# Two small writes of the expert choice, made by GpSimd in place of VectorE

## The reference

```python
def _L0_ffn_ref(x, ...):
    h = layernorm(x, ln1_scale, ln1_shift)
    x = x + attention(h, wq, wk, wv, wo, bo)      # causal softmax, 16 heads of 8
    h = layernorm(x, ln2_scale, ln2_shift)
    return x + moe_ff(h, gate_w, w1, w2, w3)

def moe_ff(x, gate_w, w1, w2, w3):
    scores = xf @ gate_w                          # 8 experts
    topk_scores, topk_idx = jax.lax.top_k(scores, 2)
    topk_probs = jax.nn.softmax(topk_scores, axis=-1)
    ...                                           # each token: its two experts, weighted

x = x + 0.5 * _L0_ffn_ref(_layernorm(x), ...)
x = x + _L0_attn_ref(_layernorm(x), ...)          # linear attention
x = x + 0.5 * _L0_ffn_ref(_layernorm(x), ...)
```

## Time and profile before

| | us |
|---|---|
| median of the runs before | 1330.87 |
| the runs | 1331.21, 1330.87, 1326.74 |
| the profiled execution | 1331.67 |
| its span | 1329.9 |

### The profile page before, as it was taken

The page is one execution under the profiler, slowest core; times in us unless marked ns, Lnnn a source line. Parts: engine busy times, 40 slices in busy tenths (PEclk is TensorE's granted clock), DMA queues, the critical chain, the costliest instruction groups (busy, mean ns, idle before and its releaser), DMA issues.

```text
span 1329.9 us, 33572 instructions
## 1 busy us (share of the span) xinstructions
PE 1012.5 (76%) x11497; PEld 753.1 (57%) x11644; DVE 1077.7 (81%) x2383; ACT 771.4 (58%) x1170; POOL 549.9 (41%) x787
## 2 busy tenths in 40 slices
PE   2789888888826998367788858998898888369980
PEld 1567666666624666245455546676676666246660
DVE  5889999999965887687588768899999998458875
ACT  1369787777724555133555534687777787245550
POOL 3402456555663666210033240034465456536660
PEclk9889999999957999566888879999999999579995
DMA  3574233225202332233222206111111010023326
GB/s 101 180 233 126 83 114 112 92 78 159 62 19 73 90 89 65 89 118 116 69 64 65 62 3 202 55 40 36 40 48 44 28 50 18 21 72 88 89 65 197
DMA packets 146339, 111.57 MB, mean 84 GB/s; under 512 B 15664, under 2 KB 140848, under 8 KB 146224
## 3 DMA queue, kind: packets, MB, share of 16 engines
q1 hardware_dynamic: 124080, 78.70, 20.4%
q0 software_dynamic: 9088, 18.76, 4.0%
q10 hardware_dynamic: 13056, 12.59, 2.7%
HBM read 43.49 MB, written 59.82 MB: 78 GB/s over the span
## 4 chain that ended last, share of the span: by engine, by line
DVE 36%; issue 21%; PE 18%; ACT 11%; POOL 8%; DMA 3%; DVEq 1%; ACTq 1%; SPq 1%; POOLq 0%
DVE negm L1031 7%; POOL ys L1434 4%; DVE negm L1035 3%; DVE p_lo L1274 3%; PE banks L422 2%; ACT pf L848 2%; DVE pf L1281 2%; DVE p_lo L1043 2%; DVE x_all L989 2%; ACT p_hi L718 2%; PE banks L457 2%; PE banks L437 1%; ACT yb L741 1%; PE banks L444 1%; DVE p_lo L1047 1%
## 5 line engine op out<-in xcount | busy, mean ns | idle before, releaser
L701 ACT ACTIVATE pf<-banks 128x1536 f32<-128x1536 f32 x128 | 185.8, 1451 | 112.8 <-PE banks L444 110.0
L1043 DVE TENSOR_TENSOR p_lo<-pf,p_hi 128x1536 f16<-128x1536 f32 x128 | 223.9, 1750 | 2.9 <-ACT p_hi L718 1.9
L1434 POOL DMA_INDIRECT ys<-y_out,dest x156 | 151.6, 972 | 115.8 <-ACT y_out L854 90.8
L718 ACT CAST p_hi<-pf 128x1536 f16<-128x1536 f32 x128 | 188.7, 1474 | 2.0
L1385 POOL DMA_INDIRECT xs<-n_all,slot x128 | 166.8, 1303 | 54.9 <-issue 37.6
L1411 POOL TENSOR_SCALAR rs<-mv 128x2 f32<-128x2 f32 x32 | 43.9, 1373 | 334.3 <-DVE mv L1096 278.1
L1031 DVE TENSOR_REDUCE negm<-banks 128x4 f16<-128x1024 f32 x128 | 156.0, 1219 | 18.2 <-PE banks L422 8.9
L444 PEld LDWEIGHTS banks<-ident,negm 128*128 128x128 f16 x1536 | 122.1, 100 | 82.6 <-issue 10.0
L437 PE MATMUL banks<-qst,kst 96*128 96x512 f16 x384 | 151.5, 395 | 2.5 <-ACT pf L701 2.5
L444 PE MATMUL banks<-ident,negm 128*128 128x128 f16 x1536 | 153.1, 223 | 0.3 <-issue 0.2
L422 PE MATMUL banks<-kst,qst 96*128 96x128 f16 x1536 | 129.8, 221 | 30.6 <-DVE negm L1031 20.2
(11 more groups left out here) (197 smaller groups left out, 2471.0 us busy)
## 6 DMA issues: line engine op xcount, KB each, us to landing
xs<-zeros SPq DMA_DIRECT2D x128, 130.0 KB
qk_d<-p_hi ACTq DMA_DIRECT2D x48, 256.0 KB, 2.2
x_nats<-xs SPq DMA_DIRECT2D x78, 130.0 KB
qst<-qk_d SPq DMA_DIRECT2D x192, 48.0 KB
kst<-qk_d SPq DMA_DIRECT2D x48, 192.0 KB
pf<-ys SPq DMA_DIRECT2D x32, 256.0 KB, 3.1
v_hl<-v_all SPq DMA_DIRECT2D x48, 136.0 KB
qk_d<-p_lo SPq DMA_DIRECT2D x96, 64.0 KB, 1.7
```

The lines of the kernel that those rows point to most:

```text
L701: nc.scalar.activation(pf[:, g % 2, :, :, :].rearrange(flat), banks_t[:, :, :].rearrange("p a b -> p (a b)"), ACT.Exp, scale=HD ** -0.5).t ...
L718: nc.scalar.copy(p_hi[:, g % 2, :, :, :].rearrange(flat), pf[:, g % 2, :, :, :].rearrange(flat))\
L1043: nc.vector.tensor_tensor(lo, pf[:, g % 2, :, :, :].rearrange(flat), hi, ALU.subtract)\
L1434: nc.gpsimd.indirect_dma_start(ys, bass.IndirectOffsetOnAxis(ap=dest[:, t % YB, h:h + 1], axis=0), y_out[:, t % YB, h, :], None).then_inc( ...
```

## The change

DVE's `choose` no longer writes `prob` and the column of `n2_all`. A new step on POOL, `keep_route`, does both: the same subtraction, and a copy from `topf` instead of `topi`. It stands directly in front of `slots` of the same batch and raises a new semaphore, `route_kept`, by one per batch over both softmax phases. Since `top` and `topf` have one buffer each, `choose` now waits until `keep_route` of the batch before has read them; the first scatter of a batch waits for its own `keep_route`; and ACT's exponential waits for `route_kept` in place of `top_in`. Where the subtraction stood in `choose`, an `apart` takes over the wait for `max`.

```diff
--- before.py
+++ after.py
@@ -233,7 +233,7 @@
         of_linear = both + "neg_in exp_in full_in k_turn_done k_nat_in state_done state_in carry_done carry_in"
         phases = [dict(shared, n=n, soft=soft, w=0 if soft else 1, back_links=4 if soft else 4,
                        **sems(n, of_soft if soft else of_linear)) for n, soft in enumerate((True, False, True))]
-        e_in = sem("e_in")
+        e_in, route_kept = sem("e_in"), sem("route_kept")
         mixtures = [dict(**sems(f"m{n}", "x_turn x_hi_in h2f_in x_lo_in up_done silu_in hid_in hid_hi_in hid_lo_in down_done "
                                 "y_in dest_in tabled added add_chain chain"), n=n, e_in=e_in,
                          x_loaded=[sem(f"x_loaded_m{n}_{i}") for i in range(XB)],
@@ -263,6 +263,10 @@
         def at_loop(i, n):
 
             return lambda d: ((4 + n + d) % RB, i + (4 + n + d) // RB)
+
+        def kept(ph, n):
+
+            return ph["n"] // 2 * B + n
 
         def fill_no(ph, b, name):
 
@@ -870,7 +874,7 @@
                     hid_high(t)
                 y_read(NTI - 2)
                 y_read(NTI - 1)
-                sc.wait_ge(phases[2 * mixtures.index(m)]["top_in"], B)
+                sc.wait_ge(route_kept, kept(phases[2 * mixtures.index(m)], B))
                 nc.scalar.activation(prob[:, :, 0], prob[:, :, 0], ACT.Exp).then_inc(m["e_in"], 1)
 
             sc.wait_ge(w_in, weights_in)
@@ -1105,17 +1109,17 @@
             def choose(ph, b):
 
                 c = Chain(ve, ph["cv_route"], b * 3)
-                two = bass.ds(2 * b, 2)
                 ve.wait_ge(ph["emptied"], fill_no(ph, b, "b8") + 1)
+                if not (isinstance(b, int) and b == 0):
+                    ve.wait_ge(route_kept, kept(ph, b))
                 apart(ve)
                 for t in range(T):
                     ins = nc.vector.max(top[:, t, :], gates[:, t, :])
                 c.link(ins)
-                nc.vector.tensor_tensor(prob[:, two, 0], top[:, :, 1], top[:, :, 0], ALU.subtract)
+                apart(ve)
                 for t in range(T):
                     ins = nc.vector.max_index(topi[:, t, :], top[:, t, :], gates[:, t, :])
                 c.link(ins)
-                nc.vector.tensor_copy(n2_all[:, two, P + 1], topi[:, :, 0])
                 c.link(nc.vector.tensor_copy(topf[:, :, :], topi[:, :, 0:2]))
                 nc.vector.tensor_tensor(onehot2[:, b, :, :, :],
                                         iota_e[:, :].unsqueeze(1).unsqueeze(1).to_broadcast([P, T, 2, E]),
@@ -1374,10 +1378,17 @@
                                                    at_slot[:, :, :, w:2 * w], ALU.add))
                 nc.gpsimd.tensor_copy(slot[:, T * b:T * (b + 1), :], at_slot[:, :, :, 0]).then_inc(ph["cp_slot"], 1)
 
+            def keep_route(ph, b):
+
+                gp.wait_ge(ph["top_in"], b + 1)
+                nc.gpsimd.tensor_tensor(prob[:, T * b:T * (b + 1), 0], top[:, :, 1], top[:, :, 0], ALU.subtract)
+                nc.gpsimd.tensor_copy(n2_all[:, T * b:T * (b + 1), P + 1], topf[:, :, 0]).then_inc(route_kept, 1)
+
             def scatter(ph, b, n):
 
                 if n == 0:
                     gp.wait_ge(ph["cp_slot"], 5 * (b + 1))
+                    gp.wait_ge(route_kept, kept(ph, b + 1))
                     gp.wait_ge(ph["n2_kept"], b + 1)
                     if ph is phases[0]:
                         gp.wait_ge(blank, SLAB * (b + 1))
@@ -1419,6 +1430,7 @@
                     if ph["soft"] and g == 0 and place > 1:
                         back_rstd(ph, b - 2)
                     if ph["soft"] and g == 1 and place > 2:
+                        keep_route(ph, b - 3)
                         slots(ph, b - 3)
                     if ph["soft"] and g == 0 and place > 3:
                         scatter(ph, b - 4, 3)
@@ -1460,13 +1472,16 @@
                         iteration(ph, b, place=b)
                     back_rstd(ph, B - 2)
                     scatter(ph, B - 4, 3)
+                    keep_route(ph, B - 3)
                     slots(ph, B - 3)
                     for n in range(4):
                         scatter(ph, B - 3, n)
                     back_rstd(ph, B - 1)
+                    keep_route(ph, B - 2)
                     slots(ph, B - 2)
                     for n in range(4):
                         scatter(ph, B - 2, n)
+                    keep_route(ph, B - 1)
                     slots(ph, B - 1)
                     for n in range(4):
                         scatter(ph, B - 1, n)
```

## The result

The changed kernel takes **1318.08 us** (median of 8 runs, 1315.05 to 1323.96). Before, measured beside it, takes 1326.78 us (median of 8, 1323.56 to 1331.21). The ratio is **0.9934**, 95% interval 0.9911 to 0.9957: 8.8 us less, at least 5.7 and at most 11.8. A second measurement in a later session gives a ratio of 0.9933 (0.9909 to 0.9958); the two medians there, 1321.95 and 1329.12 us, lie 7.2 us apart. The forecast was 5.3 us less and 1325.6 us, with a range from 1321.5 to 1331.5.

What follows compares the result with a forecast made beforehand. DVE was taken to set the softmax loop's iteration. Savings of 6.4 us (6.2 in loops, 0.2 in straight code) less 1.1 on POOL gave 5.3 us, from 1330.87 to 1325.6 us; range 1321.5 to 1331.5.

Steps and rivals of the forecast that it cites:

- GpSimd's tail: Ends of both phases, where POOL has no cover: the added pairs cost 1.1 us, bounds 0.3 to 2.4.
- VectorE sets the loop: Softmax loops: DVE waits for no other engine, so a microsecond taken from its sequence comes out of the 19.05 us iteration.
- Rival 2: Softmax loops: PE or ACT sets the iteration, which stays 19.05 us; only POOL's 1.1 us show, 1332.0 us; chance 0.09.
- Max to topf 0.83 to 0.55 us: DVE's choice in the loop, end of max to the cast topf: 0.28 us saved, bounds 0.04 to 0.40.
- The iteration of 18.77 us in place of 19.05: Sign that the forecast is right: one iteration of the softmax loop takes 18.77 us, before 19.05.
- DVE loses nothing: Loop: POOL's pair takes at_slot's place behind p_lo and is held up in its stead; p_lo keeps its 1749 ns.
- rival 1: Loop: GpSimd's later work holds up VectorE at num, up to 4.4 us, 1330.0; with cx too 1334.4; chance 0.16.
- GpSimd behind p_lo, row against rule: Loop: the trace shows POOL giving way, at_slot 1.56 us beside p_lo against 0.25; the rule would also let GpSimd block VectorE.
- the gain in the loops: DVE's choice in both softmax loops: 0.28 us saved in each of 22 iterations, 6.2 us, bounds 0.9 to 8.8.
- rival 3: Loop: the semaphore increment goes unnoticed beside the searches, 0.40 us saved per iteration, 8.8 us, time 1323.0; chance 0.19.
- Rival 4: Each choice: DVE waits for POOL at route_kept; each further microsecond of delay costs 22 us; chance 0.06.

Runs made afterwards that it cites:

- the second pair: Kernel before and changed kernel, both unaltered, profiled once more: loops 417.14 and 410.47 us; ratio 0.9933 in that later session.
- Run 2: Changed kernel with VectorE also making both writes into spare tiles: ratio to before 1.0016 with register addresses, 0.9969 with fixed addresses.
- run 5: Kernel before with six semaphore increments on VectorE ahead of its loop in both softmax phases: ratio to before 0.9996.

## Why the prediction came out too small

- **The step that failed: the base of the sum.** The prediction subtracted its 5.3 us from 1330.87, the median of the three runs shown, and its range allowed for 1.5 us of scatter between runs. Over 8 runs the median of the same kernel is 1326.78, and 1327.74 to 1329.12 in the later sessions: the base was 2 to 4 us too high. With 1326.78 in its place the same terms give 1321.5 us, and the range becomes 1317.4 to 1327.4, which holds the 1318.08. Of the 7.5 us by which 1325.6 missed, 4.1 are this and 3.4 the gain. Of the 3.4, by the first pair of profiles, 1.3 lie in the loops (7.5 us for 6.2) and 0.7 in GpSimd's tail (0.4 for 1.1). The remaining 1.4 show in no stretch; with the loops of the second pair it is 2.2.
- **VectorE sets the loop, and time taken out of it comes out of the iteration: right.** Over the kernels of the table the time follows the loops to within 4 us; no rival engine took over, not even at 18.45 us. Rival 2 is out.
- **Max to topf 0.83 to 0.55 us: right to the hundredth,** and with it that the register work behind the waits is most of it. Run 2 puts it at 0.23 to 0.24 of 0.28.
- **The iteration of 18.77 us in place of 19.05: too short for the first phase, right in the last by luck.** In the first phase it fell from 19.04 to 18.86 us, by 0.18 and not 0.28: "DVE loses nothing" beside GpSimd was wrong there, x_step and p_lo lose 0.11 us. That is rival 1's mechanism, but it struck at x_step and p_lo and not at num, where I looked. In the last phase it fell from 19.18 to 18.75 us, by 0.43: the 0.28, 0.11 by the stall that run 5 moved, and 0.03 by a shorter x_step (0.44 to 0.41). That 18.75 lies by 18.77 is chance, since the iteration started there from 19.18 and not from 19.05, which no row of before showed.
- **GpSimd behind p_lo, row against rule.** The Trainium skill ("SBUF — State Buffer", Who interferes with whom) says that a VectorE instruction with two SBUF inputs contends with a GpSimd instruction that reads SBUF, and that issue order decides who is blocked. The trace agrees for GpSimd's subtraction, which starts 0.25 us into p_lo and takes 1.60 us instead of 0.19. It doesn't agree for p_lo, which started first and takes 1.80 us beside it instead of 1.75 in the first phase.
- **Mis-sized, the gain in the loops.** The sum had 6.2 us; the profiles show 7.5, and 6.7 in the second pair. That it came so near is luck in part, since two things that the sum left out nearly cancel: the 0.11 us lost per iteration in the first phase, and the 0.14 gained in the last. No row of before could price either; nothing there shows that the program's layout costs VectorE time, and its trace has it only as a piece "issue".
- **Mis-sized, GpSimd's tail.** From the last rstd to the last scatter it is 18.15 us before (383.11 to 401.26) and 18.34 after; in the last phase 14.87 and 15.08. That is +0.4 us in place of 1.1. The timeline of GpSimd after, which answers to the earlier trace rows:

```profile
379.50 0.24 POOL L1422 TENSOR_SCALAR rs<-mv 128x2 f32<-128x2 f32 x1 [0.70 <-DVE mv L1100]
...
383.25 0.19 POOL L1384 TENSOR_TENSOR prob<-top 128x2 f32<-128x2 f32 x1
383.39 0.19 POOL L1385 COPY n_all<-topf 128x2 f32<-128x2 f32 x1
383.53 0.25 POOL L1374 TENSOR_TENSOR at_slot<-onehot,pos 128x32 f32<-128x32 f32 x1
...
389.46 1.98 POOL L1396 DMA_INDIRECT xs<-n_all,slot  x1 [0.30 <-issue]
391.46 0.21 POOL L1384 TENSOR_TENSOR prob<-top 128x2 f32<-128x2 f32 x1
...
397.84 0.96 POOL L1396 DMA_INDIRECT xs<-n_all,slot  x1 [0.30 <-issue]
```

  A pair takes 383.53 - 383.25 = 0.28 us, not 0.37: the waits cost nothing. And less of it shows. The first pair of the first phase is hidden as forecast: from rstd to the end of the long scatter it is 11.95 us before and 11.94 after. Then the first of the four last scatters starts 0.48 us later after rstd than before, but 0.29 come back, most of it in this scatter, which takes 1.05 us and before 1.31; that VectorE no longer holds it up is my reading and not shown. In the last phase the first pair goes into 0.20 us of idle time ahead of at_slot, and the second costs 0.21.
- **The chances.** The bounds of the sum (-8.7 to +1.3 us) held the gain, at their very end; I gave 0.19 to rival 3 and its 0.40 us per iteration. The last phase came out at 0.43 us, but by another cause. Rival 4, a wait at route_kept, did not occur.

What stays open: why the ends and the long stretch, in which TensorE's granted clock is 0.56 to 0.86, differ by up to 10 us between kernels, and so how much of the 8.8 us beyond the loops' 6.7 to 7.5 is more than the uncertainty of the measurement (5.7 to 11.8).

## What to carry to other kernels

Before moving a small instruction off a busy engine, look at what stands in front of it: here the two writes cost 0.04 us, and the two register instructions that computed their addresses behind waits 0.24. With fixed addresses, VectorE's stretch was nearly as short as with the move (0.59 us against 0.55). The loop written out gave more than the move (17 us against 8.8), without touching another engine. And take the base of a forecast from as many runs as there are: with runs 8 us apart, a median of three was off by half the gain.

## What the runs showed of the hardware

- Register instructions cost nothing that shows where VectorE is busy with something long (from p_lo to the next negm 1.67 us in the loop and 1.67 written out), and 0.11 to 0.12 us each between short instructions with waits: topf to onehot 0.31 us in the loop and 0.20 written out, onehot to chosen 0.34 and 0.22.
- A loop of VectorE can stall by 0.11 us at one instruction because of its place in the program: chosen to p_lo 0.22 us, or 0.11 with six instructions more ahead of the loop. With the difference moved alone, onehot to chosen is 0.10 us longer in the first phase; that this is the same kind of stall was not tried. The Trainium skill ("Advanced Engine Details and Errata", ISA Cache) says that programs are held in cache lines of 256 instructions. In the kernel before, the stall is in each iteration of the last phase's loop, while the DMA view has no instruction transfer in five of eight successive ones, so a line fetched anew in each iteration isn't the cause; what is stays open.
- VectorE's x_step, 128x256 with two inputs in SBUF, takes 0.41 or 0.42 us where GpSimd idles beside it, and 0.41 to 0.57 where GpSimd issues a scatter beside it, in one execution of one program 0.41 in some iterations and 0.49 in others.
- TensorE's granted clock over the last phase's loop was 0.97 to 0.98 in the kernels with an iteration of 19.07 us or more, 0.99 at 19.02, and 1.00, the level of 2.4 GHz, in all that are faster. The first phase doesn't bear this out: the two profiles of before have 0.98 and 1.00 there, with 19.04 and 19.03 us. So what lowers it isn't shown. In the ends of the phases the mean was 0.56 to 0.66, between the two levels of 1.2 and 2.4 GHz.
